# Numbering the expert blocks anew: 64 blocks of each half read their weights where they lie

## The reference, cut to what matters

```python
x = L0_attn_a_x                                   # 1 x 2048 tokens x 256
x = x + attn_a(layernorm(x))                      # 16 heads, causal, alibi bias
x = x + ffn(layernorm(x))
x = x + attn_b(layernorm(x))                      # 16 heads, latent K and V
x = x + ffn(layernorm(x))                         # the same weights again

def ffn(x):                                       # 64 experts, top 8, inner width 64
    logits = x @ gate_w.T
    topv, topi = top_k(logits, 8)
    W = scatter(softmax(topv), topi)              # 2048 x 64, 8 not zero in a row
    gate, up = split(einsum('nh,eih->nei', x, gu_w))
    out = einsum('nei,ehi->nh', silu(gate) * up * W[:, :, None], dp_w)
    shared = (silu(x @ sh_gate_w.T) * (x @ sh_up_w.T)) @ sh_down_w.T
    return out + sigmoid(x @ sh_gate1_w.T) * shared
```

## Time and profile before

| | us |
|---|---|
| median of 3 runs | 2060.75 (2059.88 to 2068.27) |
| the profiled execution | 2058.86 |
| its span, first to last instruction | 2054.7 |
| PE busy | 1715.9 (84%) |
| DVE busy | 1441.0 (70%) |
| ACT busy | 1110.3 (54%) |
| POOL busy | 682.0 (33%) |

### The profile page before, as it was taken

The page is one execution under the profiler, slowest core; times in us unless marked ns, Lnnn a source line. Parts: engine busy times, 40 slices in busy tenths (PEclk is TensorE's granted clock), DMA queues, the critical chain, the costliest instruction groups (busy, mean ns, idle before and its releaser), DMA issues.

```text
span 2054.7 us, 36352 instructions
## 1 busy us (share of the span) xinstructions
PE 1715.9 (84%) x12410; PEld 1071.6 (52%) x12410; DVE 1441.0 (70%) x3081; ACT 1110.3 (54%) x1975; POOL 682.0 (33%) x764
## 2 busy tenths in 40 slices
PE   6799999999877777988688999999998677779920
PEld 5445454445655656774334454544446566667710
DVE  5688989885766733886437889898848677338843
ACT  2155757667455655663122557575664566556610
POOL 6000101001366354445650001010013663544466
PEclk9788989899988899999895879898899888989965
DMA  7530404000444455665753104030004545546644
GB/s 231 164 60 2 64 2 63 2 2 7 180 170 146 157 165 151 191 196 189 213 174 57 27 2 63 2 63 1 2 7 180 180 148 162 160 146 200 201 151 117
DMA packets 127905, 225.94 MB, mean 110 GB/s; under 512 B 15364, under 2 KB 91028, under 8 KB 123444
## 3 DMA queue, kind: packets, MB, share of 16 engines
q1 hardware_dynamic: 103152, 156.49, 25.2%
q0 software_dynamic: 24576, 67.14, 12.0%
HBM read 124.20 MB, written 98.84 MB: 109 GB/s over the span
## 4 chain that ended last, share of the span: by engine, by line
PE 60%; DVE 11%; issue 9%; DMA 6%; ACT 5%; POOL 4%; another core or an unknown queue 2%; SPq 2%; DVEq 0%; ACTq 0%; POOLq 0%
PE late_banks L1659 13%; PE late_banks L1617 11%; PE late_banks L1449 9%; PE exp_banks L1645 7%; PE exp_banks L1466 6%; POOL ring_t L1043 3%; PE late_banks L1424 3%; DVE chunk_max_t L2076 3%; PE late_banks L1482 2%; PE late_banks L1623 2%; ACT probs_t L1287 2%; DVE inter_t L1957 1%; DMA expert_rows<-outs_t 1%; DVE hot_t L1778 1%
## 5 line engine op out<-in xcount | busy, mean ns | idle before, releaser
L1287 ACT ACTIVATE probs_t<-exp_banks 128x1024 f32<-128x1024 f32 (+3 forms) x640 | 538.9, 896 | 319.7 <-PE exp_banks L1645 317.0
L2076 DVE TENSOR_REDUCE chunk_max_t<-late_banks 128x1 f32<-128x512 f32 (+1 forms) x960 | 601.7, 682 | 99.2 <-PE late_banks L1617 82.6
L1125 POOL TENSOR_SCALAR_AFFINE_SELECT probs_t<-probs_t 128x512 f32<-128x512 f32 x128 | 81.5, 637 | 807.2 <-ACT probs_t L1287 807.2
L1449 PE MATMUL late_banks<-tokensT_t,fetched_t 128*128 x2048 | 315.4, 302 | 30.4 <-ACT fetched_t L1191 22.9
L1038 POOL DMA_INDIRECT ring_t<-token_rows,index_t x256 | 249.8, 976 | 213.0 <-PE late_banks L1424 144.4
L1659 PE MATMUL late_banks<-probs_t,values_t 128*32 128x512 f32 (+3 forms) x2560 | 316.8, 569 | 1.9 <-POOL probs_t L1125 1.1
L1957 DVE TENSOR_TENSOR inter_t<-late_banks,silu_t 64x256 f32<-64x256 f32 x512 | 217.7, 425 | 138.4 <-ACT silu_t L1208 107.4
L1043 POOL DMA_INDIRECT ring_t<-expert_rows,rows_of_t x256 | 244.0, 953 | 203.6 <-DVE x_sb_t L1975 138.7
L1449 PEld LDWEIGHTS late_banks<-tokensT_t,fetched_t 128*128 128x128 f32 x2048 | 270.5, 206 | 61.8 <-issue 44.3
L1466 PE MATMUL exp_banks<-fetched_t,inter_t 64*128 64x128 f32 x2048 | 197.7, 315 | 79.6 <-DVE inter_t L1957 49.5
L1617 PE MATMUL late_banks<-contextT_t,Qp_t 50*128 50x512 f32 (+7 forms) x640 | 233.7, 508 | 8.5 <-DVE chunk_max_t L2076 2.1
(11 more groups left out here) (225 smaller groups left out, 1894.9 us busy)
## 6 DMA issues: line engine op xcount, KB each, us to landing
expert_rows<-outs_t SPq DMA_DIRECT2D x256, 256.0 KB
weights_t<-in_experts SPq DMA_DIRECT2D x8, 1728.0 KB, 13.8
Qp_t<-q_rows SPq DMA_DIRECT2D x12, 768.0 KB
weights_t<-in_experts SPq DMA_DIRECT2D x4, 2112.0 KB, 7.2
q_rows<-part_hi_t SPq DMA_DIRECT2D x16, 512.0 KB, 6.3
k_rows<-part_hi_t SPq DMA_DIRECT2D x16, 512.0 KB, 6.7
Kp_t<-k_rows SPq DMA_DIRECT2D x8, 768.0 KB
q_rows<-part_lo_t SPq DMA_DIRECT2D x16, 256.0 KB, 6.9
```

What stands on the lines that cost most here:

```text
L1287: act.activation(probs[:, e % NP, 2 * p:2 * p + 2, off:QB], exp_banks[sq % 2][:, :, off:QB], ACT.Exp, scale=D ** -0.5).then_inc(exp_done, 1)
L1449: last = pe.matmul(bank[:, blk * P:(blk + 1) * P], fetched[:, n % NFETCH, blk, k * P:(k + 1) * P], tokensT[:, bass.ds(starts_of[n][blk] + ...
L2076: op = dve.tensor_reduce(chunk_max[:, b, p, chunk_row(r), chunk_col(b, r, c)], bank[:, 0:n].rearrange("q (p k) -> q p k", p=len(parts)), A ...
```

## The change

Blocks are numbered by another rule. Block e of a half (e from 0 to 63) is now the first 128 slots of expert e, or as many as it has. What experts have beyond 128 tokens makes up the other 64 blocks, the *loose* ones. So pairs 0 to 31 and 64 to 95 of a phase hold two experts known when the program is written, and PE reads their weights in `weights` itself: nothing is copied for them (`own_weights`). Pairs 32 to 63 and 96 to 127 are loose; for each of these ACT copies one block's weights and DVE the other's. That makes 128 copies on ACT and 128 on DVE in a launch, where there were 320 and 192.

The slots are ordered anew too: first what experts have up to 128, by expert, then what is beyond. The map pays for it: two more small operations in `counted`, three more in `column_keys` with `row_moves`, two more in `place_keys`, and in `bases` four small matmuls (one of 1 column, three of 64) in place of one of 512 columns. POOL sets up five more constants at the start of the phase.

The planner's rules follow: own pairs wait for no copy, but those from pair 29 on for the last slice of weights; a pair needs tile 2j+2 where it needed 2j+3; loose copies wait for all slices.

```diff
+FIXED = NEXP // 2
+MARK = 32768.0
+MAP_SETS = 13
-OTHER_FROM = NPAIR // 2
+def own_weights(n):
+    return n % NPAIR < FIXED
+def loose_no(n):
+    return n // NPAIR * (NPAIR - FIXED) + n % NPAIR - FIXED
 ...
         elif kind == "gate_up":
-            yield "fetch", n, 0.0
-            if n >= OTHER_FROM:
+            if not own_weights(n):
+                yield "fetch", n, 0.0
                 yield "other", n, 0.0
-            yield "store", h * NG + min(2 * j + 2, NG - 1), 0.0
+            elif h == 0 and 2 * j + 1 >= W_SPLITS[-2]:
+                yield "weights", PIECES - 1, LOADED
+                yield "out", LAST_LOAD, LOADED
+            yield "store", h * NG + min(2 * j + 1, NG - 1), 0.0
 ...
+        def expert_weights(n, blk):
+            if own_weights(n):
+                e = 2 * (n % NPAIR) + blk
+                return weights[:, e * EW:(e + 1) * EW]
+            return fetched[:, loose_no(n) % NFETCH, blk, :]
 ...
-                    if n >= NFETCH:
-                        act.wait_ge(down_done, f * PAIRS + n - NFETCH + 1)
-                    for blk in range(2 if n < OTHER_FROM else 1):
-                        act.activation(fetched[:, n % NFETCH, blk, :], weights[:, bass.ds(fetches[n][blk], EW)], ACT.Copy)\
-                            .then_inc(fetch_done, 1)
+                    v = loose_no(n)
+                    if v >= NFETCH:
+                        act.wait_ge(down_done, f * PAIRS + loose_pair(v - NFETCH) + 1)
+                    act.activation(fetched[:, v % NFETCH, 0, :], weights[:, bass.ds(fetches[n], EW)], ACT.Copy)\
+                        .then_inc(fetch_done, 1)
 ...
             def bases(h):
-                pe.wait_ge(count_step, 5 * (2 * f + h + 1))
-                for bank, of in ((cols_bank, tally), (rows_bank, block_rows)):
-                    pe.matmul(bank.rearrange("p (t e) -> p t e", t=HT), of[:, :],
+                pe.wait_ge(count_step, COUNT_STEPS * (2 * f + h + 1))
+                pe.matmul(cols_bank.rearrange("p (t e) -> p t e", t=HT), own[:, :],
 ...
+                pe.matmul(misc[:, OWN_AT:OWN_AT + 1], earlier[:, :], own[:, 0:1], start=True, stop=True)
+                to = misc[:, SLOTS_AT:SLOTS_AT + NEXP]
+                pe.matmul(to, own[:, :], later[:, :], start=True, stop=False, skip_group_check=True)
+                pe.matmul(to, over[:, :], earlier[:, 0:NEXP], start=False, stop=True, skip_group_check=True)
 ...
-                    pe.wait_ge(tile_stored, f * 2 * NG + h * NG + min(2 * j + 3, NG))
+                    pe.wait_ge(tile_stored, f * 2 * NG + h * NG + min(2 * j + 2, NG))
+                    for c in range(len(W_SPLITS) - 1):
+                        if n < FIXED and W_SPLITS[c] <= 2 * j + 1 and c not in landed:
+                            landed.add(c)
+                            pe.wait_ge(weights_in[c], 16 * (f + 1))
 ...
+                        expert = expert_weights(n, blk)
                         for k in range(KC):
-                            last = pe.matmul(bank[:, blk * P:(blk + 1) * P], fetched[:, n % NFETCH, blk, k * P:(k + 1) * P],
+                            last = pe.matmul(bank[:, blk * P:(blk + 1) * P], expert[:, k * P:(k + 1) * P],
 ...
             def counted(h):
+                dve.tensor_scalar(own[:, :], tally[:, :], float(P), None, ALU.min).then_inc(count_step, 1)
+                dve.tensor_scalar(over[:, :], tally[:, :], -float(P), 0.0, ALU.add, ALU.max).then_inc(count_step, 1)
 ...
+            def moved(h, which):
+                to = chosen[:, which * HT:(which + 1) * HT, :]
+                dve.scalar_tensor_tensor(out=to, in0=by_tile(map_banks(h)[1]), scalar=MARK + P, in1=each_tile(beyond[:, which, :]),
+                                         op0=ALU.is_ge, op1=ALU.mult).then_inc(moved_on, 1)
+                return to
             def column_keys(h):
-                dve.scalar_tensor_tensor(out=col_keys[:, :, :], in0=map_banks(h)[0].rearrange("p (t e) -> p t e", t=HT),
-                                         scalar=1.0, in1=mask16[:, tiles, :], op0=ALU.add, op1=ALU.mult).then_inc(keys_done, 1)
+                dve.tensor_scalar(beyond[:, 0, :], map_banks(h)[2][:, SLOTS_AT:SLOTS_AT + NEXP], -float(P), None, ALU.add)\
+                    .then_inc(beyond_set, 1)
+                to = moved(h, 0)
+                dve.tensor_tensor(col_keys[:, :, :], by_tile(map_banks(h)[0]), to, ALU.add).then_inc(keys_done, 1)
 ...
             def place_keys(h):
-                dve.scalar_tensor_tensor(out=row_keys[h][:, :, :], in0=map_banks(h)[1].rearrange("p (t e) -> p t e", t=HT),
-                                         scalar=1.0, in1=mask16[:, tiles, :], op0=ALU.add, op1=ALU.mult).then_inc(keys_done, 1)
+                to = moved(h, 1)
+                dve.tensor_tensor(to, to, each_tile(own_rows[:, :]), ALU.add).then_inc(moved_on, 1)
+                dve.tensor_tensor(row_keys[h][:, :, :], by_tile(map_banks(h)[1]), to, ALU.add).then_inc(keys_done, 1)
 ...
                 elif kind == "other":
-                    dve.wait_ge(down_done, f * PAIRS + n - NFETCH + 1)
-                    dve.tensor_copy(fetched[:, n % NFETCH, 1, :], weights[:, bass.ds(others[n], EW)]).then_inc(fetch_other, 1)
+                    v = loose_no(n)
+                    if v >= NFETCH:
+                        dve.wait_ge(down_done, f * PAIRS + loose_pair(v - NFETCH) + 1)
+                    else:
+                        dve.wait_ge(shared_down, NSHARED * (f + 1))
+                    dve.tensor_copy(fetched[:, v % NFETCH, 1, :], weights[:, bass.ds(others[n], EW)]).then_inc(fetch_other, 1)
```

160 lines of the change are left out of this document (97 added, 63 removed).

## The result

The changed kernel is slower: 2091.4 us (median of 4 runs) against 2060.3 (median of 4) of the kernel before beside it, a ratio of 1.0153 with a 95% interval of 1.0116 to 1.0190. The forecast was 2028, range 2003 to 2055.

The account below looks back on a forecast made before the run. It took pairs 0 to 31 as a chain of gather, turn, store, matmul, silu and gate with no engine full; 15 - 2 + 3 = 16 us a phase, 32 for both, gave 2028 us, range 2003 to 2055.

Parts of the forecast that it names:

- (c) and (d): Pairs 64 to 95 and 96 to 127 of a phase: together a gain of 3 us, bounds 0 and 12.
- slower: Pieces in pairs 32 to 63 and combines ahead of gate 96 hold gates: 7 us a phase lost, 2075; chance 0.06.
- PE-bound pace: Pairs 64 to 95 without DVE's copies: PE the bound, 1.73 to 1.77 us a pair for 1.90, up to 5.4.
- Map: DVE's added map operations ahead of pair 0: pair 0 comes 4.4 us late, larger bounds copy included.
- Stage (a): Pairs 0 to 31 of a phase, up to pair 32's silu: gain of 15 us, bounds 7 to 8 and 34.
- T: Time of the first half's last piece, which the last slice of weights needs: taken as 680 us.
- hole in the clock: PE's clock falls while it waits for the last slice ahead of pair 29: 5.8 us a phase, 2039; chance 0.08.
- Stage (b): Pairs 32 to 63 of a phase: 2 us lost to pieces between gates, bounds -15 and +20.
- Given back: Pairs 0 to 31 gain 12, pairs 32 to 63 lose 9, combines hold later gates: 3 us a phase, 2055; chance 0.13.
- Better: Without copies gathers quicken to near 1.3 us: 30 us a phase gained, 2001; chance 0.11.

Follow-up runs that it names:

- f3: Changed kernel with outs early (out n behind silu n+1), 44 combines ahead of gate 96: ratio 1.0097 to the kernel before.
- f4: Changed kernel with outs early and combine n of the first half behind gate 68+n, 28 ahead of gate 96: ratio 0.9881 to the kernel before.
- e7: Changed kernel with outs early and combine n of the first half behind gate 64+n, 32 ahead of gate 96: ratio 0.9896 to the kernel before.
- e10: Changed kernel, outs early, combine n behind gate 68+n, in a session where the kernel before took 4% less time: ratio 0.9916 to it.

## Why the prediction was wrong

**The step that failed is the one on (c) and (d).** It took +3 with bounds 0 and 12, and measured -27.0 in f0 and -26.9 in f1. It looked at how busy DVE and PE are, and counted the combines ahead of gate 96 rightly, but saw in them only gathers that would fit into (c), and set them off against fewer in (d). It did not ask where the outs stand in ACT's order, and it set its lower bound at nothing without a reason. In its place the runs showed two costs of the new order: outs four silus late, 8.5 us in (c) and 8.6 in (d), and combines dense ahead of the gates, 18.6 us in (c) (20.7 from f3 to f4). With both put right the same change is faster than before (e7, f4, e10). How dense combines cost that much stays open; about half of it is time in which silus are late without a cause that the profile names. The rival "slower" named the right place for half of it, combines ahead of gates in (c), at 4 us where dense combines cost 18 to 21, and added pieces in (b) that cost nothing.

**The PE-bound pace was right where nothing else held it, but seldom reached.** In e7 pairs 78 to 89 came every 1.7 us, as worked out from the earlier trace rows. Over the whole of (c), though, f4 took 63.1 us for 64.5 before on the same chip, 1.97 us a pair, and in the quick session, with no late silu, e10 took 61.5, 1.92 a pair, with PE busy for 58.0 of it at a granted clock of 1.00. The upper bound of 12 us, 56 us for (c), was out of reach: PE's own work is longer.

**Map:** forecast 4.4 late, measured 3.5 in both phases. (The order shown with the change has eight operations of 512 elements, not the seven that its text says; the forecast's count of what is new among them, two hidden and three ahead of pair 0, is right.)

**Stage (a):** forecast a gain of 15 to pair 32, map included; measured 12.7 - 3.5 = 9.2. In f1 it is 11.6 - 3.5 = 8.1. The gathers kept their pace, 1.59. The last piece and the slice behind it:

```profile
690.38 0.42 DVE L1988 TENSOR_REDUCE row_top_t<-equal_t 128x4 f32<-128x256 f32 x1
690.83 0.23 DVE L1992 TENSOR_TENSOR row_top_t<-row_top_t,route_inv_t 128x64 f32<-128x64 f32 x1
```

```profile
691.14 0.34 SPq L868 DMA_DIRECT2D weights_t<-in_experts  x1
```

Less the 7.5 us by which attention a was longer, T is 683.6 for 680, and the slice went at once, as forecast. The rest is the hole, PE in the changed kernel:

```profile
693.56 0.66 PE L1471 MATMUL late_banks<-ident_t,ring_t 128*128 128x128 f32 x2 [1.05 <-DMA ring_t<-token_rows,index_t]
699.08 1.23 PE L1516 MATMUL exp_banks<-weights_t,inter_t 64*128 64x128 f32 x8 [4.86 <-issue]
700.24 3.78 PE L1499 MATMUL late_banks<-tokensT_t,weights_t 128*128 x16
703.95 0.79 PE L1516 MATMUL exp_banks<-weights_t,inter_t 64*128 64x128 f32 x8
```

4.86 us of waiting, then 1.23 for 0.71 and 3.78 for 2 x 1.15: the rival "hole in the clock" came true at 2.0 us for two pairs, not 5.8 for four. The granted clock had fallen before that wait, at 690.5: behind the matmuls that ended at 687.3 PE had only tiles to turn and was busy for 1.3 us from 688 to 692. It was 0.50 from 692 to 704. The Trainium skill's page "TensorE: Matmul & The Clock Gate", section "HAM oscillation — how this bites in real kernels", says that a wait between bursts throttles the clock and the next burst starts cold; these rows agree.

The slice did not end that wait. DVE's first copies, which need it too, began at 698.0, but the down of 699.08 had to wait for an out, and the out for a product store. Those stores stand behind the slice on SP, which had waited for the last piece; the next one left at 691.53, and the out that needed its buffer started at 698.34:

```profile
SPq L868 <- DVEq L1996: 14.3, 1, 14.3
```

```profile
698.34 0.60 ACT L1257 ACTIVATE outs_t<-exp_banks 128x512 f32<-128x512 f32 x1 [7.74 <-DMA expert_rows<-outs_t]
```

The prediction had the stores ahead of the slice, but not those behind it. Pair 29's matmuls began at 700.24, that is 692.7 less the 7.5, where it had 686.

**Stage (b):** forecast -2, measured +6.9 and +10.8. The 11 pieces between gates were hidden, as DVE, busy for 52.3 of 95.8 us there, allowed; the numbering's gain was not seen.

**The other rivals.** "Given back" had pieces half paid in (b), which did not occur, and combines that hold the gates in (c), which did, but priced them at a gain missed and not at a loss. "Better" did not occur: the gathers did not quicken.

## What to carry to other kernels

When an order is fixed by a planner, a change of costs moves every engine's order: read where each result is drained (here, how many silus stand ahead of an out) and count what stands ahead of each gate, before trusting busy shares. With buffers two deep, a drain that stands steps late (here four) can close a loop through every engine; a single figure in the planner's book can put it there. Pacing work of the other half to one item a step, and forcing drains early, turned 1.3 to 1.5% slower into 1.2% faster: f4, 2029.1 us for 2055.0 (0.9881, 0.9839 to 0.9923), the lowest ratio of the runs here; the same kernel was 0.8% faster in the quick session (e10).
